# First chunk of a gated recurrent block by pairs of token tiles, the second chunk's mixing moved behind the first gate product

## The chip, the cores and the metric

The kernel runs on one core of a Trainium2 chip. The metric is the device time of one launch in microseconds (us), the median of the runs shown. Five engines work beside each other, each through its own instruction list in order: TensorE (PE, with its weight loads as PEld), VectorE (DVE), ScalarE (ACT), GpSimd (POOL) and SyncE (SP, which issues the DMAs). They meet at semaphores only.

## The reference

The input is x of shape 4 x 1024 x 256, all float32. Two layers follow each other:

```
t   = rmsnorm(x) * norm1_w
xb  = causal_conv4(t @ Wx) + conv_b
r,i = sigmoid(xb @ Wa), sigmoid(xb @ Wi)
a   = exp(-8 * softplus(lam) * r)
h   = scan(h' = a*h + sqrt(max(1-a*a, 1e-12)) * (i*xb))     # along the 1024 tokens
h1  = x + (h * gelu(t @ Wy)) @ Wo
u   = rmsnorm(h1) * norm2_w
x1  = layernorm(x + h1 + (gelu(u @ Wg) * (u @ Wu)) @ Wd)    # Wg, Wu: 256 x 1024
out = layernorm(x1 + relu(x1 @ W1 + b1) @ W2 + b2)          # W1: 256 x 1024
```

## The kernel before, in words

The 4096 tokens are eight chunks of 512 (four token tiles of 128, `TT`); two chunks are one sequence, so the scan state goes over from an even chunk to the odd one. A chunk goes through three stages: the mixing (normalise, transpose, products with Wx, Wa, Wi, Wy, the scan, the product with Wo, the residual h1), eight rounds of gate, up and down products (one for each 128 columns of Wg and Wu), and, ten rounds later, eight rounds of the second layer's products. Every matrix is used as a high and a low part, so each product is three matmuls. The order of work is written out by hand for each engine: first a head with the mixing of chunks 0 and 1, and then `round_of(r)`. In rounds 0 to 7 (`p == 0`, the first period) only chunk 0's gate, up and down products run; from round 8 on the mixing of chunk n is spread over the rounds of chunk n-1. The list of each engine for round 9 and all after it is the same before and after the change.

The names that the rows use: `tT` is the transposed normalised input (high and low part), `mT` the input of Wa and Wi and then of Wo, `uT` the transposed `u`, `xb` the convolved input, `xv` the input of the convolution and later the gate and the scan's result, `decay` is a, `gy` the gelu of the Wy product, `gu` the gated product that Wd takes. The letter at the end of `w_g_hi` is the matrix. The steps in short, for a chunk c: X(c), Y(c), A(c), I(c), O(c) are the products with Wx, Wy, Wa, Wi, Wo (`mix_x`, `mix_y`, `mix_decay`, `mix_input`, `mix_out`), T(c) and U(c) the eight transposes of the normalised input and of u (`transpose_t`, `transpose_u`).

`keep_running(n, bank)` issues n matmuls of the identity with itself into a bank that nobody reads, ahead of a wait. In the trace each of them makes two records. `weight_hi` and `weight_lo` make the high and the low part of a matrix in one or two pieces; `split_hi` (ACT) and `split_lo` (DVE) do the same to a transposed tile, from PSUM. ACT's functions need tables; a change of table shows as ACT_TABLE_LOAD.

Two rules of the hand-written order matter. The head's PE list before is: fillers, T(0), X(0), Y(0), T(1), A(0), I(0), X(1), Y(1), fillers, O(0), fillers, U(0), A(1), I(1), and then the rounds. And in round 7 and 8:

```python
if mixing and m == 7:
    transpose_u(n)
...
if units(r - 1):
    down(r - 1)
```

## Time and profile before

| | |
|---|---|
| median of 3 runs | 626.53 us (626.53 to 627.58) |
| the profiled execution's own time | 628.97 us |
| its span (first to last instruction) | 627.2 us |
| TensorE busy | 604.5 us, 96% of the span |
| VectorE, ScalarE, GpSimd busy | 386.0, 305.7, 204.4 us |
| mean granted TensorE clock | 0.991 |

A busy PE here counts the fillers too. The chain that ended last is PE for 85% of the span, DVE for 8%, and 2% or less of each of the others. All times in the rows further down are microseconds from the start of the span.

### The profile page before, as it was taken

The numbers are of one execution on the slowest core, as the hardware profiler recorded it, in microseconds if no ns is written. First come the engines' busy times: TensorE is split into PE (matmuls) and PEld (weight loads), VectorE is DVE, ScalarE is ACT, GpSimd is POOL, SyncE is SP. The second block draws the span as 40 slices with busy tenths as digits, with TensorE's granted clock in tenths as the row PEclk, the third lists the DMA queues.
The fourth block names the chain that finished last, engine by engine and source line by source line (L and its number), as shares of the span: only waits on it lengthen the run. The fifth ranks groups of instructions, "written<-read, shape, count | busy, mean of one in ns | idle before, by whom it ended". The sixth has DMA issues, their size and how long they took to land.

```text
span 627.2 us, 9436 instructions
## 1 busy us (share of the span) xinstructions
PE 604.5 (96%) x3633; PEld 537.1 (86%) x3633; DVE 386.0 (62%) x689; ACT 305.7 (49%) x564; POOL 204.4 (33%) x305
## 2 busy tenths in 40 slices
PE   7999988999999999999999999999999999999984
PEld 6898877788988898889888898889988898988974
DVE  5795665736485747747477566848368474562554
ACT  4774733366443754447443754438444653322341
POOL 4614117220724045140723125231531314240131
PEclk9999989999999999999999999999999999999998
DMA  8600001000000001010010101001000100010001
GB/s 276 219 2 33 1 2 34 0 1 2 33 1 1 33 1 36 2 34 0 1 34 2 34 1 34 0 1 35 2 1 0 34 2 1 0 35 1 1 33 35
DMA packets 13069, 15.69 MB, mean 25 GB/s; under 512 B 584, under 2 KB 12256, under 8 KB 13024
## 3 DMA queue, kind: packets, MB, share of 16 engines
q1 hardware_dynamic: 13024, 15.09, 7.1%
q8 instruction: 29, 0.48, 0.3%
q14 instruction: 16, 0.13, 0.1%
HBM read 10.89 MB, written 4.19 MB: 24 GB/s over the span
## 4 chain that ended last, share of the span: by engine, by line
PE 85%; DVE 8%; ACT 2%; POOL 2%; issue 2%; DMA 1%; POOLq 0%; ACTq 0%; DVEq 0%
PE psum L284 18%; PE psum L286 17%; PE psum L285 17%; PE psum L292 10%; PE psum L294 10%; PE psum L293 10%; PE psum L299 3%; DVE xb L733 1%; DVE row L808 1%; POOL normed L1047 1%; DVE xv L769 1%; DMA xs<-in_L_attn_x_dram 1%; DVE gu_raw L831 1%; POOL rstd L1016 1%; DVE sp L971 0%
## 5 line engine op out<-in xcount | busy, mean ns | idle before, releaser
L1076 POOL TENSOR_SCALAR gu_hi<-gu_raw 128x512 fp32r<-128x512 f32 x64 | 50.6, 791 | 320.0 <-DVE gu_raw L831 320.0
L841 DVE TENSOR_TENSOR hid_lo<-hid_raw,hid_hi 128x512 fp32r<-128x512 f32 x64 | 51.6, 807 | 97.1 <-ACT hid_hi L612 97.1
L608 ACT ACTIVATE hid_raw<-psum,vecs 128x512 f32<-128x512 f32 x64 | 43.9, 686 | 128.4 <-PE psum L286 128.3
L831 DVE TENSOR_TENSOR gu_raw<-psum,gu_raw 128x512 f32<-128x512 f32 x64 | 44.1, 689 | 81.5 <-PE psum L286 79.1
L292 PE MATMUL psum<-w_d_hi,gu_hi 128*128 128x256 f32 x256 | 73.2, 286 | 2.4 <-DVE gu_lo L836 2.4
L292 PE MATMUL psum<-w_hi,hid_hi 128*128 128x256 f32 x256 | 72.1, 282 | 2.4 <-DVE hid_lo L841 2.4
L294 PE MATMUL psum<-w_d_hi,gu_lo 128*128 128x256 f32 x256 | 72.4, 283 | 0.0
L293 PE MATMUL psum<-w_d_lo,gu_hi 128*128 128x256 f32 x256 | 72.1, 282 | 0.0
L294 PE MATMUL psum<-w_hi,hid_lo 128*128 128x256 f32 x256 | 71.9, 281 | 0.0
L293 PE MATMUL psum<-w_lo,hid_hi 128*128 128x256 f32 x256 | 71.8, 280 | 0.0
L599 ACT ACTIVATE gu_raw<-psum 128x512 f32<-128x512 f32 x64 | 38.0, 595 | 49.7 <-PE psum L286 49.0
L836 DVE TENSOR_TENSOR gu_lo<-gu_raw,gu_hi 128x512 fp32r<-128x512 f32 x64 | 44.7, 699 | 14.5 <-POOL gu_hi L1076 14.5
L292 PEld LDWEIGHTS psum<-w_hi,hid_hi 128*128 128x128 f32 x256 | 48.2, 188 | 6.3 <-DVE hid_lo L841 3.9
L292 PEld LDWEIGHTS psum<-w_d_hi,gu_hi 128*128 128x128 f32 x256 | 48.5, 190 | 5.1 <-DVE gu_lo L836 2.2
L284 PE MATMUL psum<-x1T_hi,w_hi 128*128 128x512 f32 x128 | 50.7, 396 | 1.5 <-DVE gu_raw L831 1.2
L284 PE MATMUL psum<-uT_hi,w_g_hi 128*128 128x512 f32 x128 | 51.0, 398 | 0.1
L293 PEld LDWEIGHTS psum<-w_lo,hid_hi 128*128 128x128 f32 x256 | 48.1, 188 | 2.4
L293 PEld LDWEIGHTS psum<-w_d_lo,gu_hi 128*128 128x128 f32 x256 | 48.5, 189 | 1.9
L286 PE MATMUL psum<-x1T_hi,w_lo 128*128 128x512 f32 x128 | 50.0, 391 | 0.0
L285 PE MATMUL psum<-x1T_lo,w_hi 128*128 128x512 f32 x128 | 50.0, 391 | 0.0
L284 PE MATMUL psum<-uT_hi,w_u_hi 128*128 128x512 f32 x128 | 49.9, 390 | 0.1
L285 PE MATMUL psum<-uT_lo,w_g_hi 128*128 128x512 f32 x128 | 50.0, 391 | 0.0
(145 smaller groups left out, 1544.8 us busy)
## 6 DMA issues: line engine op xcount, KB each, us to landing
xs<-in_L_attn_x_dram SPq DMA_DIRECT2D x8, 512.0 KB, 3.5
out_dram<-row SPq DMA_DIRECT2D x16, 256.0 KB, 2.2
raw<-in_L_ffn_W_dram SPq DMA_DIRECT2D x2, 1024.0 KB, 13.0
raw_gud<-in_L_attn_Wg_dram SPq DMA_DIRECT2D x1, 1024.0 KB, 9.0
raw_gud<-in_L_attn_Wu_dram SPq DMA_DIRECT2D x1, 1024.0 KB, 11.0
raw_gud<-in_L_attn_Wd_dram SPq DMA_DIRECT2D x1, 1024.0 KB, 13.6
raw_xyai<-in_L_attn_Wx_dram SPq DMA_DIRECT2D x1, 256.0 KB, 2.7
raw_xyai<-in_L_attn_Wy_dram SPq DMA_DIRECT2D x1, 256.0 KB, 2.9
```

Of the source, the lines that this page charges most:

```text
L284: nc.tensor.matmul(dst, w_hi[n][:, k, cols], hi[:, k, :], start=(k == 0), stop=False)
L285: nc.tensor.matmul(dst, w_hi[n][:, k, cols], lo[:, k, :], start=False, stop=False)
L286: last = nc.tensor.matmul(dst, w_lo[n][:, k, cols], hi[:, k, :], start=False, stop=(k == KD - 1))
L292: nc.tensor.matmul(dst, hi, w_hi[n][:, k, :], start=start, stop=False, skip_group_check=True)
L293: nc.tensor.matmul(dst, hi, w_lo[n][:, k, :], start=False, stop=False, skip_group_check=True)
L294: return nc.tensor.matmul(dst, lo, w_hi[n][:, k, :], start=False, stop=stop, skip_group_check=True)
L599: nc.scalar.activation(gu_raw[:, r % SLOTS, :], gate_bank(r)[:, :], ACT.Gelu_apprx_tanh).then_inc(gelu_ready, 1)
L608: nc.scalar.activation(hid_raw[:, w % SLOTS, :], bank[:, :], ACT.Relu, bias=vec("b1", m)).then_inc(relu_ready, 1)
L831: nc.vector.tensor_tensor(gu_raw[:, r % SLOTS, :], up_bank(r)[:, :], gu_raw[:, r % SLOTS, :], ALU.mult).then_inc(gu_ready, 1)
L836: nc.vector.tensor_tensor(gu_lo[:, r % SLOTS, :], gu_raw[:, r % SLOTS, :], gu_hi[:, r % SLOTS, :].bitcast(FP32), ALU.subtract).then_inc(gu ...
L841: nc.vector.tensor_tensor(hid_lo[:, w % SLOTS, :], hid_raw[:, w % SLOTS, :], hid_hi[:, w % SLOTS, :].bitcast(FP32), ALU.subtract).then_inc ...
L1076: nc.gpsimd.tensor_scalar(gu_hi[:, r % SLOTS, :], gu_raw[:, r % SLOTS, :], 1.0, 0.0, ALU.mult, ALU.add).then_inc(gu_hi_ready, 1)
```

## The change

It touches the head and rounds 0 to 8 alone. Chunk 0's x comes in two DMAs of 256 KB, and its squares, normalising, transposes and splits go by pairs of token tiles (two halves). Both normalisings of chunk 0 leave GpSimd (the first goes to VectorE, the second to ScalarE), and so do the high parts of all matrices but Wd. ScalarE does tanh, exp and squares of chunk 0 under its first table, and the gelu of Y(0) comes after the square roots. X(1) and Y(1) move into round 0, A(1) and I(1) into round 2, O(1) from round 5 to round 6, U(1) behind down(6) of round 7, and down(7) ahead of the gate product of round 8. Fillers go from 88 to 129.

```diff
@@ sync @@
-            load_x(0)
+            for q in range(PAIRS):
+                load_first_x(q)
@@ tensor, gate_up @@
                 product(gate_bank(r)[:, :], "g", m, uT_hi, uT_lo).then_inc(gate_done, 1)
+                if r == 0:
+                    mix_x(1)
+                    split_done("u")
@@ tensor, rounds @@
+                if r == KH:
+                    down(r - 1)
                 if units(r):
                     gate_up(r)
+                if r == 0:
+                    pe.wait_ge(gy_ready, KD)
+                    mix_y(1, bank=DOWN)
+                if r == 2:
+                    mix_decay(1)
+                    mix_input(1)
+                if r == 6:
+                    mix_out(1)
...
-                if units(r - 1):
+                if units(r - 1) and r != KH:
                     down(r - 1)
+                if r == 7:
+                    transpose_u(1)
@@ tensor, head @@
             pe.wait_ge(ident_ready, 1)
-            keep_running(8, SECOND)
+            keep_running(10, SECOND)
...
-            keep_running(14, SECOND)
-            transpose_t(0)
-            keep_running(5, SECOND)
+            keep_running(8, SECOND)
+            transposed_by_pairs(normed, t_ready, tT_done, MIX, (6, 9))
             split_done("x")
             mix_x(0)
-            split_done("y")
-            mix_y(0, bank=DOWN)
-            transpose_t(1)
-            keep_running(9, SECOND)
-            split_done("a", "i")
+            keep_running(36, SECOND)
+            split_done("a")
             pe.wait_ge(vecs_ready, 1)
-            mix_decay(0, bank=GATE)
+            first_decay(GATE)
+            split_done("i")
             mix_input(0, bank=SECOND)
-            mix_x(1)
-            pe.wait_ge(gy_ready, KD)
-            mix_y(1, bank=DOWN)
+            transpose_t(1)
+            split_done("y")
+            mix_y(0, bank=DOWN)
             pe.wait_ge(tanh_a_ready, KD)
             keep_running(28, GATE)
             split_done("o")
-            mix_out(0, bank=GATE)
             pe.wait_ge(tanh_i_ready, KD)
-            keep_running(24, SECOND)
-            transpose_u(0)
-            mix_decay(1, bank=SECOND)
-            pe.wait_ge(gy_ready, 2 * KD)
-            mix_input(1, bank=DOWN)
-            split_done("g", "u")
+            first_out(SECOND)
+            pe.wait_ge(gy_ready, KD)
+            keep_running(16, DOWN)
+            transposed_by_pairs(normed, u_ready, uT_done, GATE, (6, 10))
+            pe.wait_ge(uT_lo_ready, 2)
@@ tensor, new functions @@
+            def transposed_by_pairs(src, ready, done, bank, fillers):
+                for q in range(PAIRS):
+                    pe.wait_ge(ready, 2 * q + 2)
+                    for tt in (2 * q, 2 * q + 1):
+                        for f in range(KD):
+                            last = nc.tensor.transpose(pair_bank(bank, q)[:, f, (tt % 2) * P:(tt % 2 + 1) * P],
+                                                       src[:, tt, f * P:(f + 1) * P], ident[:, :])
+                    last.then_inc(done, 1)
+                    keep_running(fillers[q], DOWN)
+            def first_decay(bank):
+                for k in range(KD):
+                    pe.wait_ge(xb_lo_ready, k + 1)
+                    for m in range(KD):
+                        last = product_step(psum[bank + m][:, :], "a", m, k, mT_hi, mT_lo)
+                        if k == KD - 1:
+                            last.then_inc(wa_done, 1)
@@ scalar, head @@
+            gelu_y(0, bank=DOWN)
+            weight_hi("o")
             hy_hi(0)
...
+            split_hi(tT_hi, tT_done, tT_hi_ready, 1)
+            square_first_h1()
+            weight_hi("u", "n2")
+            first_norm_u()
+            split_hi_by_pairs(uT_hi, GATE, uT_done, uT_hi_ready)
@@ vector, rounds 7 and 8 @@
-                if r == 7:
-                    split_lo(uT_lo, uT_hi, uT_hi_ready, uT_lo_ready, n)
                 gate_lo(r)
...
+                if r == 7:
                     weight_lo("1", ks=[0])
...
+                if r == KH:
+                    split_lo(uT_lo, uT_hi, uT_hi_ready, uT_lo_ready, 1)
+                    weight_lo("1", ks=[1])
```

The first place is TensorE, from the end of O(0) to the first round. Before, the fillers and the eight transposes of u are followed by A(1) (`mT` with `w_a`):

```order
L470 MATMUL psum<-ident 128x128 x24
L299 MATMUL psum<-ident,normed 128x128 x8
L284 MATMUL psum<-mT_hi,w_a_hi 128x512
L285 MATMUL psum<-mT_lo,w_a_hi 128x512
L286 MATMUL psum<-mT_hi,w_a_lo 128x512
L284 MATMUL psum<-mT_hi,w_a_hi 128x512
```

After the change the same place has the second pair's transposes, fillers, the gate product of round 0 (`uT` with `w_g`) and then X(1) (`tT` with `w_x`):

```order
L332 MATMUL psum<-ident,normed 128x128 x4
L540 MATMUL psum<-ident 128x128 x10
L305 MATMUL psum<-uT_hi,w_g_hi 128x512
L306 MATMUL psum<-uT_lo,w_g_hi 128x512
L307 MATMUL psum<-uT_hi,w_g_lo 128x512
L305 MATMUL psum<-uT_hi,w_g_hi 128x512
L306 MATMUL psum<-uT_lo,w_g_hi 128x512
L307 MATMUL psum<-uT_hi,w_g_lo 128x512
L305 MATMUL psum<-tT_hi,w_x_hi 128x512
L306 MATMUL psum<-tT_lo,w_x_hi 128x512
```

So the gate product is reached with four products of chunk 1 (X, Y, A, I) still to do.

The second place is VectorE at rounds 7 and 8, before the change, from gu of round 7 to gu_lo of round 8 (psum5 and psum1 are the banks of the up products):

```order
L831 TENSOR_TENSOR gu_raw<-psum5,gu_raw 128x512
L722 TENSOR_TENSOR uT_lo<-psum6,uT_hi 128x512
L722 TENSOR_TENSOR uT_lo<-psum7,uT_hi 128x512
L836 TENSOR_TENSOR gu_lo<-gu_raw,gu_hi 128x512
L831 TENSOR_TENSOR gu_raw<-psum1,gu_raw 128x512
L722 TENSOR_TENSOR tT_lo<-psum6,tT_hi 128x512
```

And the same place after it:

```order
L948 TENSOR_TENSOR gu_raw<-psum5,gu_raw 128x512
L953 TENSOR_TENSOR gu_lo<-gu_raw,gu_hi 128x512
L969 TENSOR_TENSOR w_1_lo<-raw_1,w_1_hi 128x1024
L826 TENSOR_TENSOR uT_lo<-psum6,uT_hi 128x512
L826 TENSOR_TENSOR uT_lo<-psum7,uT_hi 128x512
L969 TENSOR_TENSOR w_1_lo<-raw_1,w_1_hi 128x1024
L948 TENSOR_TENSOR gu_raw<-psum1,gu_raw 128x512
L826 TENSOR_TENSOR tT_lo<-psum6,tT_hi 128x512
```

The low part of u, for which round 8's gate product waits, now stands behind gu_lo of round 7 and a piece of W1.

## Rows read from the trace of the kernel before

**Rows 1.** The page: the span, and busy time of the engines.
```profile
span 627.2 us, 9436 instructions
PE 604.5 (96%) x3633; PEld 537.1 (86%) x3633; DVE 386.0 (62%) x689; ACT 305.7 (49%) x564; POOL 204.4 (33%) x305
```

**Rows 2.** Windows, PE alone: start:end, length, busy (records), granted clock, DMA share, GB/s.
```profile
84.00:85.00 1.00, 1.00 (x7) 0.50 0.00 0
120.00:200.00 80.00, 79.91 (x474) 1.00 0.02 8
```

**Rows 3.** Timeline, PE, rounds 4 to 9: the waits, and X(2) at 106.08.
```profile
82.83 0.38 PE L292 MATMUL psum<-w_d_hi,gu_hi 128*128 128x256 f32 x1 [1.83 <-DVE gu_lo L836]
...
97.95 1.09 PE L299 MATMUL psum<-ident,normed 128*128 128x128 f32 x8 [2.17 <-POOL normed L1047]
...
100.62 0.50 PE L284 MATMUL psum<-uT_hi,w_g_hi 128*128 128x512 f32 x1
...
103.46 1.04 PE L299 MATMUL psum<-ident,normed 128*128 128x128 f32 x8
104.26 0.37 PE L292 MATMUL psum<-w_d_hi,gu_hi 128*128 128x256 f32 x1
...
106.08 0.51 PE L284 MATMUL psum<-tT_hi,w_x_hi 128*128 128x512 f32 x1
```

**Rows 4.** Timeline, PE: start, length, instruction, idle before and who ended it.
```profile
1.51 3.66 PE L470 MATMUL psum<-ident 128*128 128x128 f32 x16 [1.51 <-POOL ident L1118]
...
35.22 6.41 PE L470 MATMUL psum<-ident 128*128 128x128 f32 x56
...
42.18 0.36 PE L292 MATMUL psum<-w_o_hi,mT_hi 128*128 128x256 f32 x1 [0.55 <-DVE mT_lo L784]
...
45.13 5.07 PE L470 MATMUL psum<-ident 128*128 128x128 f32 x44
...
57.98 0.39 PE L284 MATMUL psum<-uT_hi,w_g_hi 128*128 128x512 f32 x1
...
60.70 0.39 PE L284 MATMUL psum<-uT_hi,w_g_hi 128*128 128x512 f32 x1
...
68.41 0.28 PE L292 MATMUL psum<-w_d_hi,gu_hi 128*128 128x256 f32 x1
...
69.82 0.40 PE L284 MATMUL psum<-uT_hi,w_g_hi 128*128 128x512 f32 x1
```

**Rows 5.** Timeline, DVE: scan, the low part for O(0), a convolution step, one piece of W2.
```profile
37.01 2.33 DVE L769 TENSOR_TENSOR_SCAN xv<-decay,inp 128x512 f32<-128x512 f32 x2
...
40.68 1.36 DVE L784 TENSOR_TENSOR mT_lo<-gy,mT_hi 128x512 fp32r<-128x512 f32 x2
...
93.78 1.22 DVE L852 TENSOR_TENSOR w_lo<-raw,w_hi 128x1024 fp32r<-128x1024 f32 x1
...
117.38 1.40 DVE L733 SCALAR_TENSOR_TENSOR xb<-xv,vecs,xb 128x512 f32<-128x512 f32 x2
```

**Rows 6.** Timeline, ACT: table loads and the work around them; the last row is W1's high part.
```profile
28.39 1.28 ACT L557 ACT_TABLE_LOAD   x1
29.69 1.52 ACT L557 ACTIVATE decay<-decay,half_c 128x512 f32<-128x512 f32 x2
31.12 1.14 ACT L564 ACTIVATE xv<-decay 128x512 f32<-128x512 f32 x2
...
65.90 2.00 ACT L622 ACTIVATE w_hi<-raw 128x1024 fp32r<-128x1024 f32 x2
```

**Rows 7.** The chain that ended last, ACT: the four squares of h1 of chunk 0.
```profile
46.05 0.92 ACT inp L591 x4
```

**Rows 8.** Timeline, POOL: u of chunk 1, then the rms of chunk 2 and gu_hi of round 7.
```profile
96.05 1.84 POOL L1047 TENSOR_SCALAR normed<-h,rstd 128x256 f32<-128x256 f32 x4 [0.17 <-POOL rstd L1016]
...
98.26 1.01 POOL L1016 TENSOR_TENSOR rstd<-rstd,minus_half 128x4 f32<-128x4 f32 x1
99.25 0.62 POOL L1076 TENSOR_SCALAR gu_hi<-gu_raw 128x512 fp32r<-128x512 f32 x1
```

More of the change, by code:

```diff
@@ L138, in up_bank, with squares_done, half, pair_bank @@
             return psum[SECOND + 1] if r < KH and r % 2 else psum[UP]
+        def squares_done(c):
+            return c + 2
+        def half(q):
+            return slice(q * (T // 2), (q + 1) * (T // 2))
+        def pair_bank(bank, q):
+            return psum[bank + q][:, :].rearrange("p (f t) -> p f t", f=KD)
+        def taps_done(c, step, m):
+            return m * LOOKBACK + step + 1 if c == 0 else 6 * c + step * KD + m + 1
         def second_bank(c):
@@ L157, in griffin_mlp_kernel @@
         x_loaded = [sem(f"x_loaded{i}") for i in range(2)]
+        x0_loaded = [sem(f"x0_loaded{q}") for q in range(PAIRS)]
         out_stored = [sem(f"out_stored{i}") for i in range(2)]
@@ L316, in transpose_t @@
                     pe.wait_ge(tap_done, 2)
-                elif c >= 2:
+                else:
                     pe.wait_ge(uT_lo_ready, 2 * c)
@@ L440, in round_of @@
                     mix_decay(n)
-                if mixing and m == 7:
+                if mixing and m == 7 and p >= 1:
                     transpose_u(n)
@@ L463, in round_of @@
                     mix_y(n)
-                if mixing and m == 5:
+                if mixing and m == 5 and p >= 1:
                     mix_out(n)
@@ L507, in _, with square_first_x @@
         def _(act):
+            def square_first_x():
+                for q in range(PAIRS):
+                    act.wait_ge(x0_loaded[q], DMA)
+                    for tt in (2 * q, 2 * q + 1):
+                        last = nc.scalar.activation(flat(decay)[:, tt * D:(tt + 1) * D], xs[0][:, tt, :], ACT.Square,
+                                                    accum_out=ss1[:, tt:tt + 1])
+                    last.then_inc(x_squared, 1)
             def square_x(c):
-                act.wait_ge(x_loaded[c % 2], (c // 2 + 1) * DMA)
-                if c >= 1:
-                    act.wait_ge(rms1_ms, c)
+                act.wait_ge(x_loaded[c % 2], (c // 2 + c % 2) * DMA)
+                act.wait_ge(rms1_ms, squares_done(c - 1))
                 if c >= 2:
@@ L523, in split_hi, with split_hi_by_pairs @@
                     nc.scalar.activation(dst[:, f, :], psum[MIX + f][:, :], ACT.Copy).then_inc(ready, 1)
+            def split_hi_by_pairs(dst, bank, done, ready):
+                for q in range(PAIRS):
+                    act.wait_ge(done, q + 1)
+                    nc.scalar.activation(dst[:, :, half(q)], pair_bank(bank, q), ACT.Copy).then_inc(ready, 1)
             def conv_start(c, m):
@@ L635, in round_of @@
                     split_hi(x1T_hi, x1T_done, x1T_hi_ready, p - 1)
-                if mixing and m == 6:
+                if mixing and m == 6 and p >= 1:
                     square_h1(n)
@@ L865, in first_period @@
                 n = 1
-                if r == 1:
+                if r == 3:
                     room(n)
-                if r == 6:
+                if r == 4:
+                    for k in range(KD):
+                        scan_input(n, k)
+                if r == 7:
                     for q in range(PAIRS):
@@ L969, in _ @@
             lam_stepped(nc.vector.tensor_scalar(poly, z, 1.0 / 17.0, None, ALU.mult))
-            for odd in range(15, 1, -2):
+            for odd in range(15, 5, -2):
+                lam_stepped(nc.vector.scalar_tensor_tensor(poly, poly, 1.0 / odd, z, ALU.add, ALU.mult))
+            for step in range(LOOKBACK):
+                convolve_half(0, step, 0)
+            convolve_half(0, 0, 1)
+            weight_lo("a")
+            xb_lo(0, [0])
+            convolve_half(0, 1, 1)
+            convolve_half(0, 2, 1)
+            weight_lo("i")
+            xb_lo(0, [1])
+            for odd in range(5, 1, -2):
                 lam_stepped(nc.vector.scalar_tensor_tensor(poly, poly, 1.0 / odd, z, ALU.add, ALU.mult))
```

225 lines of the change are left out of this document (131 added, 94 removed).

## The prediction, before the changed kernel was run

> **What bounds the kernel now.** I read the page first: TensorE is busy for 96% of the span [rows 1], so an edit pays only where TensorE waits, works at the low clock or runs fillers. The windows come next: from 120 us on TensorE is full at the full clock (79.91 of 80 us in the one shown) [rows 2]. All that can change lies ahead of that, and since the engines' lists are equal from round 9 on, one number decides: when X(2), the last step of round 8, begins. It is 106.08 now [rows 3]. Then the timeline of TensorE: the first gate product begins at 57.98 [rows 4], with all mixing of chunks 0 and 1 done but O(1). From there to X(2) are 48.1 us.
>
> Prices from that timeline. A gate and an up product, twelve matmuls, take 60.70 - 57.98 = 2.72 us, and so does each of X, Y, A and I. A down product takes 69.82 - 68.41 = 1.41, and O 45.13 - 42.18 = 2.95 [rows 4]. Eight transposes take 104.26 - 103.46 = 0.80 [rows 3]. A filler takes 6.41/28 = 0.229, and 3.66/8 = 0.457 in the cold start [rows 4]. So of the 48.1 us, 9 x 2.72 + 8 x 1.41 + 2.95 + 1.6 = 40.3 are work. The other 7.8 are the waits of 1.83 and 2.17 [rows 3] (about 0.2 more each until the first record after them is under way), some shorter ones, and about 1.7 us that matmuls lost in the stretch at clock 0.50 [rows 2] that follows the wait of 1.83.
>
> **When the first gate product starts after the change.** TensorE's own list: start 1.51, ten fillers 3.66 + 0.46, the transpose of the vectors 0.1, 23 fillers 5.27, two pairs of transposes 0.8, X(0) 2.72: 14.5. Then 36 fillers 8.24, A(0) and I(0) 5.44, T(1) 0.8, Y(0) 2.72, 28 fillers 6.41: 38.1; with some 0.1 for each of four first matmuls after a wait, 38.5. These fillers run whether or not the data are there, so this is a floor. Are the data later than it? Ahead of A(0) they aren't: the convolution's six steps (0.70 each [rows 5]), four splits of 0.6 to 0.7 and the weights' splits that now stand between them bring the second half of `mT` at about 21.9, and the fillers end near 23. The two DMAs of x, the pairs' squares and the normalising on VectorE are covered in the same way: TensorE's fillers hold the first pair's transposes until 7.6 and the second's until 9.5, and without that cover the chain would be ready some 1.5 us earlier, no more. Ahead of O(0): tanh of A(0) is done at about 26.6, exp to squares 1.43, squares to tanh about 1.0, two tanh 1.1 (as two squares, 1.14), load to next 29.69 - 28.39 = 1.30, two square roots 1.2 [rows 6]: 32.7. Then VectorE: 0.7, scan 2.33, the low part of Wo 0.7, gy 0.7, then high and low part 0.6 + 0.7 [rows 5]: 38.4. So data and fillers meet, and O(0) starts at 38.6, where it is 42.18 now [rows 4]. The gelu of Y(0) behind the second load is covered by the scan. The removed loads, 2 x 1.28 [rows 6], are in this gain and not beside it.
>
> O(0) ends at 41.5, 16 fillers reach 45.2. The second half of h1 is there at 42.4, its two squares end at 43.4 (0.92 for four records [rows 7]), and then ScalarE makes the high part of Wu, 2.00 us by the same shape of W1 [rows 6], before it normalises u. The first pair is ready at 46.2, so TensorE waits 1.0. Then 0.4 + 6 fillers 1.37 + 0.4 + 10 fillers 2.29: the gate product starts at **50.8, 7.2 us sooner**.
>
> **What that costs behind it.** X(1), Y(1), A(1) and I(1), 4 x 2.72 = 10.9 us, used to be done by then, two of them in the very time in which chunk 0's tanh, exp and scan ran. That time is now filled by fillers (129 for 88, 41 x 0.229 = 9.4 us), and the products stand in rounds 0 and 2. So X(2) starts at 50.8 + 40.3 + 10.9 = 102.0 plus W, the waits from the first gate product on. Break-even is W = 4.1. I walk through the rounds with these prices:
> - A(1), round 2. TensorE gets there at 65.8. VectorE can begin the second convolution step only after gu(1) (62.5), then 1.35, gu_lo(1) 0.6, 1.35, and the high and low part of two halves: 67.2. Wait 1.5. Queued behind it are I(1), D(1) and rounds 3 on.
> - D(4), round 5. ScalarE after A(1): load, exp, tanh, squares, load, gelu(3), load, roots, load, gelu(4), which ends at 82.0; VectorE then gu(4), the scan 2.33 and gu_lo(4): 85.8 for 85.15. Wait 0.65.
> - O(1), round 6: gated, gu(5), gu_lo(5), low part of gy: 90.4. Wait 0.5.
> - D(7), now ahead of the gate product of round 8. U(1) ends at 99.65. GpSimd has u normalised at 98.6 (0.9 squares, 1.4 rms, 1.84 [rows 8]), then the rms of chunk 2 in 1.27 and gu_hi(7) 0.62 [rows 8]; VectorE 0.65: 101.3. Wait 1.6, where the present wait of 2.17 ahead of U(1) goes away.
> - Gate product of round 8. VectorE has a piece of W1 (1.22 [rows 5]) and then the low part of u (1.3) after gu_lo(7): 103.8 for 102.7. Wait 1.1.
> - X(2). From T(2) to X(2) are 106.08 - 103.46 = 2.62 [rows 3] through ScalarE and VectorE, of which T(2) takes 0.80. Now D(7) stands in that hole; it has been done already. Wait 1.8.
>
> W = 7.15, and X(2) starts at 109.2: **3.1 us later**. Bounds of W: from below, only the hole that no other work can fill, X(2)'s 1.8, and half of the rest, 4.5, +0.5 us; from above, one more stretch at clock 0.50 like the 1.7 us of before and convolution or scan steps slowed beside GpSimd (POOL) by 1 us, +5.8. I take my walk's value, since it uses the shape's own rows. Of fixed costs, the second x DMA delays SP's later issues by about 0.45 us; the weights are used more than 2 us after that. Behind round 9 the lists are equal and TensorE is full [rows 2], so nothing gives the 3.1 back. The profiled execution took 628.97 us in all, 1.8 over its span, and would become 632.1; its distance from the median of 626.53 stays, so the median becomes **629.6**.
>
> **A rule of the skill against the row.** The load at 28.39 is followed by exp at 29.69 [rows 6], 0.02 us after the load's end. The Trainium skill, ScalarE: Activation LUTs, section What ACT_TABLE_LOAD costs, adds a drain of about 1.38 us to each load of about 1.28. By the row the chain to O(0) holds two loads of 1.30; by the page it would be 2.8 us longer, O(0) at about 41.2 and the median near 632. The trace doesn't agree: no drain stands between load and exp. I go by the row.
>
> **The rivals.**
> - *Slower, as above* (0.54): 629.6, from +1.3 to +5.
> - *Slower by more* (0.14): the low clock returns. Six waits of 0.5 to 1.8 us stand in 45 us; after the 1.83 us the granted clock fell to 0.50 [rows 2], after the 2.17 us it didn't. One or two falls at 1.7 each: 631.3 to 633.
> - *Faster* (0.20): the deferred products act as slack. While TensorE does 10.9 us of mixing in rounds 0 and 2, VectorE and ScalarE run ahead, so that the waits inside rounds 2 to 8 shrink. It decides at W below 4.1; for example with W of 2.6, X(2)'s hole and 0.8 more, X(2) starts at 104.6, and the median is 625.0. For it speaks that the waits of 1.83 and 2.17 come from work packed tightly around the scan; against it that D(7) is placed where gu_hi(7) on GpSimd can't be ready.
> - *No change* (0.12): the gain at the head and the loss behind it meet, W of 3 to 5: 626.5.
>
> **How the numbers follow.** 629.6 is the likeliest case's value. What a measurement here can tell from no change is about 0.2%, 1.25 us. Slower by over that holds 0.68, within it 0.12, faster 0.20. The range reaches down to 624.8, which leaves out a fast tail of 0.15, and up to 632.8. The likeliest case's own range is 628 to 631.5.
>
> **What would show each step.** Right: the first gate product near 50.8 and X(2) near 109.2; A(0) straight after its fillers near 23; O(0) near 38.6; waits ahead of A(1), D(7), the gate product of round 8 and X(2). Wrong: fillers that end before the data (the head later than 50.8, and all else with it); a wait ahead of D(7) under 0.5; no wait at A(1). The prediction fails if the waits after the first gate product sum to under 4 us, or if the gate product starts before 48.

## The result, and the profile after

The changed kernel takes **633.03 us** (median of 4, 632.23 to 633.65) against 626.53 (median of 4, 626.0 to 627.58): a ratio of 1.0091, 95% interval 1.0067 to 1.0114. It is slower. The two medians lie 6.5 us apart where 3.1 were forecast, and 633.03 is 0.2 us above the range's upper end of 632.8. The ratio on record is not the quotient of the two medians (1.0104); by it the loss is 5.7 us, which puts the changed kernel at 632.2. Three of the four executions behind 626.53 are among the quickest that the kernel before has: over the 74 executions of it that were timed beside the experiments the median is 627.7, and against that the loss is 5.4 us. The section on the prediction comes back to this.

Two rows of the page, to be read against [rows 1]:

```profile
span 631.9 us, 9603 instructions
PE 611.4 (97%) x3715; PEld 544.2 (86%) x3715; DVE 385.6 (61%) x692; ACT 311.3 (49%) x575; POOL 194.6 (31%) x293
```

TensorE is busy 6.9 us longer, in a span that is 4.7 us longer, with 82 records more: what was added is 41 fillers, two records each. The timeline of TensorE has the milestones. They are A(0), O(0), U(0)'s first half, the first gate product, and then the waits: A(1), D(4), D(7), the gate product of round 8, X(2). They answer to [rows 3, 4].

```profile
23.68 0.48 PE L305 MATMUL psum<-mT_hi,w_a_hi 128*128 128x512 f32 x1
...
39.05 0.36 PE L316 MATMUL psum<-w_o_hi,mT_hi 128*128 128x256 f32 x1
...
46.77 0.66 PE L332 MATMUL psum<-ident,normed 128*128 128x128 f32 x4 [1.03 <-ACT normed L684]
...
51.20 0.47 PE L305 MATMUL psum<-uT_hi,w_g_hi 128*128 128x512 f32 x1
...
68.21 0.50 PE L305 MATMUL psum<-mT_hi,w_a_hi 128*128 128x512 f32 x1 [1.71 <-DVE mT_lo L861]
...
87.07 0.38 PE L316 MATMUL psum<-w_d_hi,gu_hi 128*128 128x256 f32 x1 [0.66 <-DVE gu_lo L953]
...
102.60 0.39 PE L316 MATMUL psum<-w_d_hi,gu_hi 128*128 128x256 f32 x1 [1.38 <-DVE gu_lo L953]
...
105.13 0.50 PE L305 MATMUL psum<-uT_hi,w_g_hi 128*128 128x512 f32 x1 [0.83 <-DVE uT_lo L826]
...
110.59 0.50 PE L305 MATMUL psum<-tT_hi,w_x_hi 128*128 128x512 f32 x1 [1.57 <-DVE tT_lo L826]
```

The gate product starts 6.8 us sooner than before, X(2) 4.5 us later. From X(2) to the end of the span are 631.9 - 110.59 = 521.3 us, where they were 627.2 - 106.08 = 521.1. In every run below this difference lies between 521.1 and 521.5, so for each profiled execution the place of X(2) is the whole result.

### The profile page after: what moved, and what is told of

It is laid out like the page before. It is cut to its first block, busy times and chain, and to the rows that moved or that the text cites. A ratio compares the mean times of both kernels' runs of the same rounds, so it can differ in the third digit from the quotient of the medians.

```text
span 631.9 us, 9603 instructions
## 1 busy us (share of the span) xinstructions
PE 611.4 (97%) x3715; PEld 544.2 (86%) x3715; DVE 385.6 (61%) x692; ACT 311.3 (49%) x575; POOL 194.6 (31%) x293
## 4 chain that ended last, share of the span: by engine, by line
PE 87%; DVE 5%; issue 2%; ACT 2%; POOL 2%; POOLq 0%; ACTq 0%; DVEq 0%
PE psum L305 17%; PE psum L307 17%; PE psum L306 17%; PE psum L316 10%; PE psum L318 10%; PE psum L317 10%; PE psum L540 4%; PE psum L323 3%; DVE xb L850 1%; DVE row L925 1%; POOL gu_hi L1210 0%; DVE gu_raw L948 0%; DVE gu_lo L953 0%; DVE hid_lo L958 0%; POOL ln_rstd L1196 0%
## 5 line engine op out<-in xcount | busy, mean ns | idle before, releaser
L1210 POOL TENSOR_SCALAR gu_hi<-gu_raw 128x512 fp32r<-128x512 f32 x64 | 52.0, 812 | 313.8 <-DVE gu_raw L948 313.8
L307 PE MATMUL psum<-uT_hi,w_u_lo 128*128 128x512 f32 x128 | 49.9, 390 | 0.0
```

The costliest lines, as they stand in the source:

```text
L307: return nc.tensor.matmul(dst, w_lo[n][:, k, cols], hi[:, k, :], start=False, stop=(k == KD - 1))
L1210: nc.gpsimd.tensor_scalar(gu_hi[:, r % SLOTS, :], gu_raw[:, r % SLOTS, :], 1.0, 0.0, ALU.mult, ALU.add).then_inc(gu_hi_ready, 1)
```

## The experiments

Twelve kernels. Their medians stand beside that of the kernel before, timed with them on the same chip (626.3 to 627.9, by how many of its executions fell into each of three groups that come further down). The ratio is the one on record, not the quotient of the medians. The milestones are those of each one's profiled execution:

| run | first gate product | X(2) | span | median (low to high, n) | before there | ratio, 95% |
|---|---|---|---|---|---|---|
| before | 57.98 | 106.08 | 627.2 | 626.53 (626.0 to 627.58, 4) | | |
| after | 51.20 | 110.59 | 631.9 | 633.03 (632.23 to 633.65, 4) | 626.53 | 1.0091 [1.0067, 1.0114] |
| e1, old order of rounds 7 and 8 | 50.66 | 108.34 | 629.8 | 631.09 (630.9 to 631.57, 4) | 626.77 | 1.0062 [1.0040, 1.0084] |
| e2, fewer fillers | 48.60 | 108.01 | 629.4 | 631.15 (630.73 to 631.89, 4) | 626.77 | 1.0063 [1.0041, 1.0086] |
| e3, X(1), Y(1) back in the head | 51.31 | 106.20 | 627.6 | 629.92 (629.25 to 630.58, 10) | 626.77 | 1.0045 [1.0032, 1.0058] |
| e4, only the first ten fillers | 49.40 | 111.06 | 632.4 | 633.74 (631.62 to 634.22, 4) | 626.77 | 1.0097 [1.0069, 1.0125] |
| e5, e1 + e3 + fewer fillers | 50.68 | 104.47 | 626.0 | 627.68 (627.25 to 627.88, 10) | 627.73 | 1.0002 [0.9992, 1.0013] |
| e6, all mixing but O(1) back | 55.43 | 102.03 | 623.4 | 626.07 (624.84 to 627.91, 12) | 627.73 | 0.9982 [0.9969, 0.9995] |
| e7, two loads more | 53.25 | 112.61 | 633.9 | 635.76 (635.14 to 637.83, 4) | 627.73 | 1.0140 [1.0114, 1.0166] |
| e8, e6 with VectorE reordered | 55.29 | 103.75 | 625.1 | 625.27 (624.11 to 627.16, 10) | 627.86 | 0.9977 [0.9961, 0.9992] |
| e9, e6 with its hole filled | 56.00 | 104.16 | 625.5 | 626.91 (626.23 to 627.29, 10) | 627.86 | 0.9991 [0.9981, 1.0001] |
| e10, before with holes filled | 58.13 | 107.35 | 628.6 | 629.60 (628.91 to 630.41, 6) | 627.86 | 1.0036 [1.0021, 1.0050] |
| e11, before, gu_lo(4) first | 56.41 | 103.77 | 624.9 | 628.29 (626.66 to 629.83, 10) | 627.86 | 1.0008 [0.9993, 1.0023] |
| e12, e8 with POOL reordered | 52.44 | 97.22 | 618.6 | 620.62 (620.38 to 620.97, 6) | 626.33 | 0.9896 [0.9878, 0.9914] |

### e1: rounds 7 and 8 in the old order

```diff
-                if r == KH:
-                    down(r - 1)
...
-                if units(r - 1) and r != KH:
+                if units(r - 1):
                     down(r - 1)
...
+                if r == 7:
+                    split_lo(uT_lo, uT_hi, uT_hi_ready, uT_lo_ready, 1)
                 gate_lo(r)
...
                 if r == KH:
-                    split_lo(uT_lo, uT_hi, uT_hi_ready, uT_lo_ready, 1)
                     weight_lo("1", ks=[1])
```

> The changed kernel with its order of rounds 7 and 8 undone: D(7) stands behind T(2) again, and VectorE makes the low part of u ahead of gu_lo(7) and of W1's piece. Theory (the new order opens three holes): the waits of 1.38 ahead of D(7), 0.83 ahead of round 8's gate product and 1.57 ahead of X(2) go, one wait of about 1.5 ahead of that gate product comes in their place; X(2) starts at 108.2 for 110.59, and the median falls by 2.4 us to 630.6. Rival (the holes are only the sight of a chain on GpSimd, and any order waits for it): X(2) within 0.5 of 110.6, median 633.

X(2) comes at 108.34. The waits from D(7) on, 1.38 + 0.83 + 1.57, become 1.57, 0.48 and 0.16:

```profile
102.19 0.49 PE L305 MATMUL psum<-uT_hi,w_g_hi 128*128 128x512 f32 x1 [1.57 <-DVE uT_lo L823]
...
105.70 1.07 PE L323 MATMUL psum<-ident,normed 128*128 128x128 f32 x8 [0.48 <-POOL normed L1157]
...
108.34 0.50 PE L305 MATMUL psum<-tT_hi,w_x_hi 128*128 128x512 f32 x1 [0.16 <-DVE tT_lo L823]
```

From A(1) to X(2) are 40.67 us instead of 42.38. So the new order of rounds 7 and 8 costs 1.7 us; the rest of the 2.25 is a head that came 0.54 sooner in this execution. The theory held, with X(2) at 108.34 for 108.2 and the median at 631.09 for 630.6, and the rival did not. D(7) is worth more in the hole between T(2) and X(2) than ahead of the gate product.

### e2: fewer fillers

```diff
-            transposed_by_pairs(normed, t_ready, tT_done, MIX, (6, 9))
+            transposed_by_pairs(normed, t_ready, tT_done, MIX, (6, 7))
...
-            keep_running(36, SECOND)
+            keep_running(32, SECOND)
...
-            transposed_by_pairs(normed, u_ready, uT_done, GATE, (6, 10))
+            transposed_by_pairs(normed, u_ready, uT_done, GATE, (6, 7))
```

> The changed kernel with 9 fillers fewer (9 to 7 ahead of X(0), 36 to 32 ahead of A(0), 10 to 7 ahead of the first gate product). Theory (these three groups end after their data, so TensorE's fillers set the head): A(0) starts 1.3 earlier at 22.6, the first gate product at 49.2 to 49.6 for 51.20, X(2) at about 108.8 for 110.59, median 631.2. Rival (the data come when the fillers end; or the clock drops as soon as a gap opens): no step earlier than in the changed kernel by more than 0.5, or a stretch at granted clock 0.50, and a median of 633 or more.

Nine fillers out, 2.06 us by the row of 0.229 [rows 4], and the gate product and X(2) both come 2.6 sooner (48.60, 108.01); the other 0.5 is the start's own spread (X(0) lies at 11.65 in e3, 12.37 in e1 and 12.89 in after, with the same fillers ahead). The median fell by 1.9 us. The head was bound by fillers, as the prediction read it, and what it had in surplus went into the total one to one.

### e3: X(1) and Y(1) in the head again

```diff
@@ gate_up and rounds, r == 0 @@
-                    mix_x(1)
...
-                    mix_y(1, bank=DOWN)
@@ tensor, head @@
             mix_x(0)
-            keep_running(36, SECOND)
+            split_done("y")
+            mix_y(0, bank=DOWN)
+            keep_running(24, SECOND)
...
-            keep_running(28, GATE)
+            keep_running(11, GATE)
+            mix_x(1)
+            pe.wait_ge(gy_ready, KD)
+            mix_y(1, bank=DOWN)
+            keep_running(4, GATE)
```

(Semaphore waits are left out here. On ScalarE and VectorE the splits of `tT`, the gelu of Y(1) and the low parts of Wo and Wg move ahead with them. Y(0) takes the place of 12 fillers behind X(0); X(1) and Y(1) take its old place and that of 13 more.)

> The changed kernel with Y(0) in the place of 12 of the fillers behind X(0), and X(1) and Y(1) back in the head, in the place of the fillers ahead of O(0) (their inputs' splits and outputs' copies move with them; the low parts of Wo and Wg go into VectorE's idle time before the scan). A(1) and I(1) stay in round 2. Theory (5.44 us of work that had filled a hole now stands behind the first gate product): O(0) at 39.6, gate product about 52.1, 0.9 later than in the changed kernel, but X(2) at 105.3, 5.3 earlier; median 627.7. Rival (the waits behind the gate product swallow what is moved out): X(2) within 1.5 of 110.6, median 631.5 or more.

O(0) and the gate product stay (39.10, 51.31), X(2) comes at 106.20, 4.4 us sooner. The two products are 5.4 us of work; they stand in the head at no cost to it, and about 1.0 us of them is lost again, most of it to new waits in rounds 0 and 1 (0.27 for `w_u_lo`, 0.91 for `gu_lo`). It is the largest part of the change that was run by itself. The median fell by less than the profile, 3.1 us to 629.92, where 627.7 was expected: the profiled execution of after is the slowest of its four (633.65), that of e3 the second of its ten (629.38).

### e4: only the first ten fillers

```diff
-                for _ in range(times):
+                for _ in range(times if times == 10 and bank == SECOND else 0):
```

> The changed kernel with only its first ten fillers; the other 119 are left out. Theory (fillers only hold the clock up, and three groups overshoot): TensorE shows the granted clock 0.50 in parts of the head, the first gate product comes at 48.5 to 51, and X(2) at 108.5 to 111. Rival A (fillers are pure cost, the clock plays no part): gate product at 48.0 or earlier and X(2) at 107.5 or earlier, clock 1.00 throughout. Rival B (the head hangs on the clock): gate product later than 52.

The windows (start:end, length, then the busy time of PE, PEld, DVE, ACT, POOL, then the granted clock):

```profile
10.00:20.00 10.00, 6.00 (x16) 4.44 (x16) 7.11 (x17) 6.05 (x16) 0.58 (x2) 0.67 1.03 381
20.00:30.00 10.00, 10.00 (x42) 7.71 (x40) 5.23 (x14) 9.06 (x14) 3.56 (x6) 0.82 0.59 205
30.00:40.00 10.00, 4.00 (x19) 3.77 (x18) 7.44 (x12) 5.62 (x10) 0.71 (x1) 0.69 0.01 2
```

X(0) starts at 9.82, 3.1 us sooner than with fillers, and A(0) at 18.40; but the products then run at a mean clock of 0.7 to 0.8, the gate product comes at 49.40, only 1.8 sooner, A(1) at 68.69 and X(2) at 111.06. Here the data bound the head: TensorE waits 4.00, 6.00, 4.69 and 1.46 us ahead of A(0), O(0), U(0) and the gate product. What this chain has gained by 49.40 it loses in rounds 0 and 1, where the clock is still low. The forecast of the theory held nearly (X(2) at 111.06 for 108.5 to 111), and both rivals fell. So the fillers can't go: they hold the clock. What is open to saving is their surplus (e2), or the place where work could stand instead (e3).

### e5: e1, e3 and fewer fillers together

The edit is that of e1 and e3, with 9, 24 and 10 fillers of e3 made 7, 19 and 7.

> Three edits to the changed kernel together: X(1), Y(0) and Y(1) in the holes of the head (as in the run that did this alone), the old order of rounds 7 and 8, and fewer fillers (9 to 7, 24 to 19, 10 to 7). From the single runs: the gate product at 49.6 (51.3 less 1.05, as far as the data ahead of A(0) allow, less 0.7), X(2) 106.2 - 1.75 - 2.3 = 102.1, span 521.3 more, 623.4, median 625.2. Theory (the parts are independent terms of one chain): X(2) within 1.0 of 102.1. Rival (they share one hidden limit): X(2) at 104 or later.

It is back at the time of before (1.0002), but 2.5 us above what was expected. The rival held, with X(2) at 104.47. The trimmed fillers brought the gate product to 50.68 and nothing to A(1): 63.78 for 63.86 in e3. VectorE was busy without a break there, and the gain fell into the first of these two waits, which is 0.27 in e3; the second is 0.91 there.

```profile
53.12 0.47 PE L305 MATMUL psum<-uT_hi,w_u_hi 128*128 128x512 f32 x1 [0.81 <-DVE w_u_lo L962]
...
58.38 0.36 PE L316 MATMUL psum<-w_d_hi,gu_hi 128*128 128x256 f32 x1 [0.94 <-DVE gu_lo L948]
```

```profile
50.00:60.00 10.00, 8.26 (x45) 6.59 (x44) 10.00 (x12) 3.09 (x4) 2.02 (x2) 1.00 0.01 2
```

The first fence is PE's timeline, the second a window. Its third busy time is VectorE's: 10.00 of 10, as in e3. The 1.7 us of e1 came in full.

### e6: all mixing of chunk 1 but O(1) back in the head

Chunk 0's mixing stays as the change has it. X(1), Y(1), A(1) and I(1) stand ahead of the first gate product, rounds 0 to 8 are those of before, and the high parts of Wu and Wd are made by POOL. Seven fillers fewer stand ahead of A(0) (9 to 7, 24 to 19).

```diff
@@ tensor, head, from O(0) on, against e3 @@
             first_out(SECOND)
-            keep_running(16, GATE)
+            keep_running(12, GATE)
             pe.wait_ge(gy_ready, 2 * KD)
-            transposed_by_pairs(normed, u_ready, uT_done, GATE, (6, 10))
+            transposed_by_pairs(normed, u_ready, uT_done, GATE, (6, 0))
+            pe.wait_ge(h1_ready, 2)
+            mix_decay(1, bank=SECOND)
+            mix_input(1, bank=DOWN)
+            split_done("g", "u")
```

> The changed kernel's head for chunk 0 (pairs, one table session, high parts off GpSimd but Wu's and Wd's), but all of chunk 1's mixing but O(1) back in the head's holes: X(1) and Y(1) ahead of O(0), A(1) and I(1) between the transposes of u and the first gate product, and rounds 0 to 8 as in the kernel before. Theory (the displaced 10.9 us are what made the change a loss, its head is a gain): O(0) at 38.1 for 42.2 before, gate product at 51.6 for 57.98, with the same work done; X(2) at 98.0 to 99.5, span 619.3 to 620.8, median 621 to 622.6, 5 us under the kernel before. Rival (the holes of the head are now too short, so the products delay U(0) and the gate product as much as they save): gate product at 55 or later, X(2) at 103 or later, median 626 or more.

It is faster than before by a little (0.9982, interval 0.9969 to 0.9995), but the forecast of 621 to 622.6 was missed: the gate product (55.43) and the median (626.07) are where the rival put them, and X(2) is at 102.03 instead of 98 to 99.5, since O(0) came at 41.98. X(1) waited 2.83 us, and ran at half the clock until 37.4. PE's row, three of DVE's timeline and one of POOL's:

```profile
33.99 0.62 PE L305 MATMUL psum<-tT_hi,w_x_hi 128*128 128x512 f32 x1 [2.83 <-DVE tT_lo L816]
```

```profile
25.01 3.34 DVE L957 SCALAR_TENSOR_TENSOR w_g_lo<-raw_gud,vecs,w_g_hi 128x1024 fp32r<-128x1024 f32 x2
...
29.78 2.96 DVE L863 SCALAR_TENSOR_TENSOR inp<-inp,xb 128x512 f32<-128x512 f32 x2
32.66 1.28 DVE L816 TENSOR_TENSOR tT_lo<-psum,tT_hi 128x512 fp32r<-128x512 f32 x2
```

```profile
25.11 4.47 POOL L1202 TENSOR_SCALAR w_u_hi<-raw_gud,vecs 128x1024 fp32r<-128x1024 f32 x2
```

While POOL makes its two high parts (25.11 to 32.2), the gate's input takes VectorE 2.96 us for its two instructions; in e8, after POOL is done (30.76), the same two take 1.28:

```profile
30.98 1.28 DVE L863 SCALAR_TENSOR_TENSOR inp<-inp,xb 128x512 f32<-128x512 f32 x2
```

The Trainium skill, GPSIMD Engine Reference, section Specifications, says that POOL shares its SBUF interface with VectorE and contends with VectorE's instructions that have two SBUF inputs or run in a 2-port mode. This instruction has two, and the trace agrees. `tT_lo`, one of whose inputs lies in PSUM, took 1.27 us in e8 beside POOL's high part of Wd, and so lost nothing.

### e7: two table loads more

```diff
             tanh_decay(0, bank=GATE)
+            act.preload_act_table(ACT.Gelu_apprx_tanh)
             act.wait_ge(consts_ready, 1)
```

> The changed kernel with ScalarE's one table session of chunk 0 broken: the gelu table is loaded between tanh and exp of the decay, and the first table again ahead of exp. Two loads more on the chain from A(0) to O(0). Theory (that chain is the bound ahead of O(0), each load costs its record's 1.30 us): O(0) at 41.6 for 39.05, X(2) at 113.2, median 635.6. By the Trainium skill, ScalarE: Activation LUTs, What ACT_TABLE_LOAD costs, with its drain: O(0) at 44.4, median 638.3. Rival (the fillers ahead of O(0) cover it): O(0) at 39.1, median 633.

ACT's timeline, and then PE's:

```profile
26.71 1.28 ACT L802 ACT_TABLE_LOAD   x1
28.00 1.28 ACT L634 ACT_TABLE_LOAD   x1
29.30 1.52 ACT L634 ACTIVATE decay<-decay,half_c 128x512 f32<-128x512 f32 x2
```

```profile
23.06 0.48 PE L305 MATMUL psum<-mT_hi,w_a_hi 128*128 128x512 f32 x1
...
41.12 0.35 PE L316 MATMUL psum<-w_o_hi,mT_hi 128*128 128x256 f32 x1 [2.45 <-DVE mT_lo L902]
```

From load to load are 1.29 us, from load to exp 1.30. O(0) moved by 2.1 us, the gate product and X(2) by 2.0, but the head of this execution also began 0.6 sooner. From A(0) to O(0) are 18.06 us for 15.37 in after, 2.7 more, and the median moved by 2.7 to 635.76 (forecast 635.6). So two loads cost what their two records show, and the data and the fillers meet so closely ahead of O(0) that the fillers cover none of it.

### e8: e6 with VectorE's order mended

```diff
@@ vector, head @@
-            weight_lo("g", "n2")
+            weight_lo("g", "n2", [0])
             room(0)
-            gated_input(0)
             split_lo(tT_lo, tT_hi, tT_hi_ready, tT_lo_ready, 1)
+            gated_input(0)
...
             hy_lo(0)
+            weight_lo("g", "n2", [1])
@@ vector, round 4 @@
                     gated(n)
-                    hy_lo(n)
...
                 gate_lo(r)
+                if r == 4:
+                    hy_lo(n)
@@ tensor, ahead of O(0) @@
-            keep_running(4, GATE)
+            keep_running(18, GATE)
```

> The kernel of e6 with VectorE's order mended: in e6 X(1) waited 2.83 us for tT_lo(1), which stood behind w_g_lo (3.34 us for its two pieces) and the gate's input (2.96 us). Here tT_lo(1) stands ahead of the gate's input, the second piece of w_g_lo behind mT_lo(0), gu_lo(4) ahead of mT_lo(1), and 14 fillers more stand ahead of O(0). Theory (VectorE's order made the hole, and the hole the half clock): X(1) at 31.2 to 31.6 with no wait and at full clock, O(0) at 39.6, the first gate product at 53.0, D(4) without its 1.84 us, X(2) at 98.5, the median at 621.7 to 622.8. Rival (VectorE beside POOL is the bound whatever the order, since it was busy without a break from 24.3 to 40.1 in e6): O(0) stays near 41.5, X(2) near 100.7, the median at 624.5.

X(1) started at 31.11 with no wait and at full clock, as expected. The rest missed: 625.27 for 621.7 to 622.8. The 14 added fillers are two records each [rows 4], twice what the forecast counted, so 36 records held TensorE until 41.8, though `mT_lo`(0) was done at 38.4. O(0) is thus where the rival put it, but by the fillers and not by VectorE. And D(4)'s wait shrank from 1.84 to 0.44 us only for U(1)'s to grow from 2.19 to 3.15. The granted clock is 0.50 from 92.3, still inside that wait, to 99.1. PE's row, and POOL's timeline ahead of it:

```profile
93.39 1.97 PE L323 MATMUL psum<-ident,normed 128*128 128x128 f32 x8 [3.15 <-POOL normed L1169]
```

```profile
87.95 0.62 POOL L1198 TENSOR_SCALAR gu_hi<-gu_raw 128x512 fp32r<-128x512 f32 x1 [5.55 <-DVE gu_raw L938]
88.65 0.70 POOL L1135 TENSOR_SCALAR rstd<-ss 128x4 f32<-128x4 f32 x1
89.44 1.87 POOL L1138 TENSOR_TENSOR rstd<-rstd,minus_half 128x4 f32<-128x4 f32 x1
91.48 1.85 POOL L1169 TENSOR_SCALAR normed<-h,rstd 128x256 f32<-128x256 f32 x4 [0.18 <-POOL rstd L1138]
```

The squares of h1 were done at 86.7. POOL had been idle for 5.55 us and stood at gu_hi(6), which waits for gu_raw(6); rstd, which could have run, was queued behind it.

### e9 and e10: filling the holes behind which the clock fell

```diff
@@ e9, against e6, ahead of X(1) @@
-            keep_running(11, GATE)
+            keep_running(35, GATE)
@@ e10, against before: ahead of X(0), and ahead of D(4) @@
-            keep_running(5, SECOND)
+            keep_running(21, SECOND)
...
+                if r == 5:
+                    keep_running(16, MIX)
                 if units(r - 1):
                     down(r - 1)
```

> The kernel of e6 with 24 fillers more ahead of X(1), where it waited 2.83 us and then ran at clock 0.50 from 34.0 to 37.4. No operation of the work moves. Theory (the idle time lowers the clock, and that is what put e6 behind its forecast): X(1) still at 34.0, but at full clock, Y(1) done at 39.4, O(0) at 40.2 (VectorE's mT_lo(0) bounds it), X(2) at 100.2, mean clock 0.996 or more, the median at 623.6 to 624.3. Rival (the clock falls there for another reason, or mT_lo(0) moves too): the median stays at 626.0.

> The kernel before with fillers in the two holes behind which its profiled execution shows clock 0.50: 16 more ahead of X(0) (a wait of 2.00 us at 11.66) and 16 ahead of D(4) (a wait of 1.83 us at 81.00). Nothing else moves. Theory (the executions of before at clock 0.991 to 0.994 are those in which one or both stretches at 0.50 fell, 1.5 and 1.7 us each; that is what was taken for a constant distance from the median in the prediction): every execution at 0.996 or more and within 626.0 to 626.8, median 626.3, where before has a second group at 627.6 to 629.2. Rival (the groups come from elsewhere): the same spread and median as before.

Both had the same slip in the number of fillers: 48 records in e9 and 32 at each place in e10, 5.5 and 3.7 us, in holes of 2.83, 2.00 and 1.83. So X(1) of e9 came at 36.17, and e10's A(0) at 24.34 and its D(4) at 84.48. e9 is at the time of before within its interval and e10 is slower, and neither time tells anything of the theory; but the clock does. In both profiled executions the filled stretches ran at 1.00, and the clock fell behind a later hole. In e9 this is D(4)'s wait of 1.83; in e10 it is U(1)'s of 2.19:

```profile
82.00:84.00 2.00, 2.00 (x11) 2.00 (x10) 1.26 (x3) 0.00 (x0) 0.62 (x1) 0.50 0.00 0
```

```profile
98.00:100.00 2.00, 1.92 (x11) 1.92 (x11) 0.41 (x1) 0.79 (x2) 1.83 (x5) 0.61 0.03 8
100.00:102.00 2.00, 2.00 (x11) 2.00 (x11) 1.76 (x3) 0.41 (x1) 2.00 (x5) 0.54 0.00 0
```

In the profiled execution of before, U(1)'s wait of 2.17 was followed by no fall, and in that of e6 neither D(4)'s 1.84 nor U(1)'s 2.19 was. It looks as if the fall were handed on to a later hole, but these are single executions of kernels whose executions differ. By mean clock e6 has two executions at 0.993 or 0.994, seven at 0.991 and three at 0.988, and e9 has all ten at 0.993 or 0.994. The profiles put one fall at 0.993 or 0.994 and two at 0.991. By that reading the filled hole of e9 took away a fall in most executions, and one stayed in each. That is argued from mean clocks and not shown. The part of the theory that every execution of e10 would be at 0.996 or more fell: three of six are at 0.994, and 1.3 us longer than the other three. Whether the filling changed anything there can't be told from six.

### e11: the kernel before with gu_lo(4) ahead of mT_lo(1)

The edit is the one of round 4 in e8.

> The kernel before with one edit on VectorE: gu_lo(4) ahead of mT_lo(1) in round 4 (0.68 us ahead of 1.47 us). Theory: D(4)'s wait falls from 1.83 to 0.4 us, the half clock behind it goes, O(1) finds mT_lo(1) ready, X(2) at 104.7 less what the clock gives (1.7 us against the profiled execution of before), the median 1.4 to 2.5 us under before: 625.0 to 625.6. Rival (the time is given back at the wait ahead of D(7) or of X(2), which POOL's normed and VectorE's tT_lo set): the median unchanged to within 0.5 us.

The theory fell and the rival held, though the time came back at U(1) and not at D(7) or X(2): D(4)'s wait went from 1.83 to 0.45, U(1)'s from 2.17 to 3.14, and the median didn't move (1.0008). The clock fell behind the longer wait:

```profile
94.46 1.79 PE L299 MATMUL psum<-ident,normed 128*128 128x128 f32 x8 [3.14 <-POOL normed L1048]
...
96.00:98.00 2.00, 2.00 (x12) 2.00 (x11) 1.77 (x3) 0.63 (x2) 2.00 (x5) 0.50 0.00 0
```

Its profile also prices a fall of the clock. The head is the same as before up to round 4, but no stretch at clock 0.50 stands behind X(0), which starts at 13.26 for 13.66; A(0) is at 22.64, where it was at 24.21. The fall behind X(0) cost the profiled execution of before 1.2 us, and with the later start its head took 1.6 us longer.

### e12: POOL's rstd first

Against e8: the fillers ahead of O(0) again 4 instead of 18, and on POOL

```diff
+                if r == 6:
+                    rms(1, ss2, h1_squared, rms2_ms, rstd2, rms2_rstd)
                 if r < UNITS:
                     gate_hi(r)
```

(and the same rms is left out of its old place, ahead of the normalising of u).

> The kernel of e8 with two edits. The 14 fillers that e8 had too many ahead of O(0) are taken out again (each is two records of 0.115 us in the trace, so they cost 3.2 us where 1.6 was meant, and TensorE came to O(0) 3 us behind mT_lo(0)). And POOL computes rstd of chunk 1's h1 ahead of gu_hi(6): its squares were done at 86.7, gu_hi(6) waited until 87.95 for gu_raw(6), and rstd stood behind it until 88.65, so that U(1) waited 3.15 us. Theory (U(1)'s wait is POOL's order, and the half clock follows the longest idle stretch): O(0) at 38.9, the first gate product at 52.4, U(1)'s wait 1.0 to 1.5, no stretch at clock 0.50 (mean 0.996), X(2) at 96.9 to 98.5, the median at 620.5 to 622. Rival (the chain h1, squares, rstd, normed keeps its length and the wait only moves to uT_lo ahead of the gate product of round 8): O(0) at 38.9, X(2) near 100.8, the median at 623 to 624.

The median is 620.62, 1.0% under before (0.9878 to 0.9914), and all six executions lie within 0.6 us. The rows of PE and then of POOL:

```profile
38.33 0.36 PE L316 MATMUL psum<-w_o_hi,mT_hi 128*128 128x256 f32 x1
...
52.44 0.39 PE L305 MATMUL psum<-uT_hi,w_g_hi 128*128 128x512 f32 x1
...
89.07 1.09 PE L323 MATMUL psum<-ident,normed 128*128 128x128 f32 x8 [1.77 <-POOL normed L1170]
...
97.22 0.50 PE L305 MATMUL psum<-tT_hi,w_x_hi 128*128 128x512 f32 x1 [0.15 <-DVE tT_lo L816]
```

```profile
84.08 1.02 POOL L1138 TENSOR_TENSOR rstd<-rstd,minus_half 128x4 f32<-128x4 f32 x1
85.08 0.62 POOL L1199 TENSOR_SCALAR gu_hi<-gu_raw 128x512 fp32r<-128x512 f32 x1
85.68 3.34 POOL L1170 TENSOR_SCALAR normed<-h,rstd 128x256 f32<-128x256 f32 x4
```

No stretch is at clock 0.50, and only U(1)'s wait of 1.77 lies above what was expected (1.0 to 1.5). Of the 6.5 us by which X(2) is sooner than in e8, 2.85 lie ahead of the gate product (the surplus fillers, and a start that came 0.4 sooner), 1.4 are the wait of U(1), and the rest, some 2.2, is put down to the half clock behind it. In medians the gain is 4.7 us, since the profiled execution of e8 is a slow one of it; against e8's three executions at a mean clock of 0.996 (624.1 to 624.3) it is 3.6. The two edits weren't run apart.

## Why the prediction was right in sign and short in size

**The head.** Right. A(0) followed its fillers at 23.68 (forecast near 23), O(0) came at 39.05 (38.6), TensorE waited 1.03 us for u (1.0), the gate product came at 51.20 (50.8). That it is right to 0.4 us is in part luck: X(0) came at 12.89, 1.1 us later than in the sum (11.8), and 64 fillers gave 0.5 us back, since they took 0.221 us each and not 0.229. X(0) varies by as much between runs with the same fillers (e2). e2 shows that fillers bound the head, e4 that they must be there, e7 that a load costs 1.30 us. The cover was a little thicker than the 1.5 us of the prediction: without fillers (e4) the low part of `mT` is ready 1.9 us sooner ahead of A(0) and 2.8 us sooner ahead of O(0). By the drain that the Trainium skill adds (ScalarE: Activation LUTs, What ACT_TABLE_LOAD costs), e7 would have moved by 5.3 us and not by 2.7.

**What it costs behind the head.** Right in kind, and short by 1.0 us. Each wait stands where it was put and for the reason given: A(1) 1.71 (forecast 1.5), D(4) 0.66 (0.65), D(7) 1.38 (1.6), gate product of round 8 0.83 (1.1), X(2) 1.57 (1.8); O(1)'s 0.5 has no bracket. Their sum, 6.15, is under the 7.15 of W; yet W came out at 110.59 - 51.20 - 40.3 - 10.9 = 8.2. The term that was too small is the time around a wait. The prediction had noted some 0.2 us until the stream is under way, and left it out of W. The starts of the records have it:

```profile
66.11 0.39 PE L307 MATMUL psum<-uT_hi,w_u_lo 128*128 128x512 f32 x1
68.21 0.50 PE L305 MATMUL psum<-mT_hi,w_a_hi 128*128 128x512 f32 x1 [1.71 <-DVE mT_lo L861]
...
91.11 0.39 PE L307 MATMUL psum<-uT_hi,w_u_lo 128*128 128x512 f32 x1
91.63 0.39 PE L316 MATMUL psum<-w_o_hi,mT_hi 128*128 128x256 f32 x1
```

Without a wait the next record starts 0.23 us after the one at 66.11. A(1) starts 2.10 after it, so 0.16 are lost beside the 1.71, and its twelve matmuls then take 2.90 for 2.72, 0.18 more. Taken in this way the five waits lose 0.23 to 0.35 us each beside their brackets, 1.5 in all. O(1) loses 0.3, which is its wait, and the first gate product and small differences 0.2. That is the 2 us. In the data chain, A(1) came 1.0 later than forecast, 0.4 of it from the head and the rest from VectorE, whose convolution steps beside gu_hi took 1.76 and not 1.35 to 1.40 [rows 5]:

```profile
57.64 1.76 DVE L850 SCALAR_TENSOR_TENSOR xb<-xv,vecs,xb 128x512 f32<-128x512 f32 x2
...
63.08 1.76 DVE L850 SCALAR_TENSOR_TENSOR xb<-xv,vecs,xb 128x512 f32<-128x512 f32 x2
...
65.37 1.40 DVE L850 SCALAR_TENSOR_TENSOR xb<-xv,vecs,xb 128x512 f32<-128x512 f32 x2
66.80 1.35 DVE L861 TENSOR_TENSOR mT_lo<-xb,mT_hi 128x512 fp32r<-128x512 f32 x2
```

So X(2), forecast at 109.2, came at 110.59: 1.4 us of the error, 0.4 from the head and 1.0 from W. A further 0.2 lies behind X(2) (521.3 for 521.1 us).

**"Its distance from the median of 626.53 stays."** Here the prediction was furthest off. The profiled execution of before was 2.4 us over its median, and that distance was no constant: it had a mean clock of 0.991, with two stretches at 0.50, behind D(4)'s wait of 1.83 [rows 2, 3] and behind X(0)'s of 2.00, here with a window behind it (PE alone):

```profile
13.66 0.47 PE L284 MATMUL psum<-tT_hi,w_x_hi 128*128 128x512 f32 x1 [2.00 <-DVE tT_lo L722]
```

```profile
16.00:17.00 1.00, 1.00 (x4) 0.50 1.08 360
```

The 74 executions of before that were timed beside the experiments fall into groups: 31 of 626.0 to 626.8 us at a mean clock of 0.996 or 0.997, 34 of 627.2 to 628.3 at 0.993 or 0.994, 9 of 628.9 to 629.2 at 0.991. The profiled one, 628.97, belongs to the last. The changed kernel has fillers or work in both of these holes, and its longest wait is 1.71: its four executions are at 0.996 to 0.998. Its profile stands 0.6 us over its median. So 4.7 us between two profiles are 6.5 between two medians, and 1.8 of the 3.4 us missing come from here. This part is no cost of the change but the luck of two samples. The trace that was read is one of the slowest executions of the kernel before, and the median of four was on the quick side: by the 627.7 of all 74 the distance would have been 1.3 us, and 0.7 instead of 1.8 would be missing here. The two stretches at 0.50 were there to be seen in the trace; how often they come was not.

**The rivals.** *Slower by more* (631.3 to 633) had the value but the wrong mechanism: no low clock came in after. *Faster* by slack of the deferred products has nothing for it: the waits stand where the walk put them, and X(1) and Y(1) back in the head's holes make the kernel faster (e3). For A(1) and I(1) this is not shown apart, since e6 has other edits beside them.

**Where the expected gain went.** The gate product is 6.8 us sooner, but 10.9 us of mixing that had stood in the head's holes stand behind it now, and the holes hold fillers in its place. e6 and e12 have both: the pair-wise head of the change, and the mixing in its holes.

## What to carry to other kernels

Where a head is a chain of dependent steps with fillers between them, a milestone that comes sooner because work was moved behind it is no gain; ask what stands in the holes afterwards, and put the next chunk's products there first and fillers second. Ahead of a comparison with a median, ask where in its own spread the profiled execution lies, by its mean clock and by each stretch at half clock, and correct for it before adding a difference. When waits are added up, add some 0.3 us beside each, as these traces have it. And when a wait is taken away, read the next wait on the same engine: here 1.4 us taken at D(4) came back as 1.0 at U(1) (e8, e11), and in e12, where the idle engine that fed U(1) did its work in another order, that wait shrank too.
